# Local attention: GpSimd normalises q as well as k, and VectorE's product of the maxima with q's reciprocal norm is gone

## What is computed

```python
def l2norm(t):
    return t / jnp.clip(jnp.linalg.norm(t, axis=-1, keepdims=True), 1e-12)

h = shift_token(x)
q, k, v = jnp.split(h @ wqkv, 3, axis=-1)        # 8 heads of 64
q = l2norm(q) * qs
k = l2norm(k) * ksc
q, k = rotary_xpos(q, k)
bq = q.reshape(b, h, w, WINDOW, d) * QK_SCALE    # windows of 64 tokens
sim = einsum(bq, own and previous window of k)   # causal mask, 128 keys at most
attn = jax.nn.softmax(sim, axis=-1)
x = x + (attn @ v) @ wo
```

## Time and profile before

| | us |
|---|---|
| median of 3 runs | 1655.27 (1651.87 to 1656.19) |
| the profiled execution, its own time | 1658.24 |
| its span in the trace | 1656.5 |
| PE busy | 1525.9 (92%) |
| DVE busy | 1137.0 (69%) |
| ACT busy | 1083.1 (65%) |
| POOL busy | 517.0 (31%) |

### The profile page before, as it was taken

How to read it: one execution, slowest core, us unless ns; L and a number is a source line. 1 busy time by engine, 2 the same in 40 slices (tenths; PEclk the granted TensorE clock), 3 DMA queues, 4 the chain that set the end, 5 groups by cost and what they waited for, 6 DMA issues and landing times. The chain is left out here.

```text
span 1656.5 us, 30452 instructions
## 1 busy us (share of the span) xinstructions
PE 1525.9 (92%) x10190; PEld 1033.3 (62%) x10190; DVE 1137.0 (69%) x2336; ACT 1083.1 (65%) x2499; POOL 517.0 (31%) x476
## 2 busy tenths in 40 slices
PE   7999999999979999999979999996999888999986
PEld 6777777777667888888854333333566555566654
DVE  2666666666658777777787788864677654767755
ACT  2555555555567888888856577754777755777751
POOL 1222222222232112222110000015767633776732
PEclk9999999999979999999987799978999999999998
DMA  7000000000011221221100000000000000000000
GB/s 236 2 2 0 0 0 0 0 0 0 1 49 57 77 76 64 76 76 55 59 1 1 1 1 1 1 1 1 1 1 1 1 1 0 1 2 1 1 1 26
DMA packets 18993, 36.35 MB, mean 22 GB/s; under 512 B 5764, under 2 KB 11008, under 8 KB 16704
## 3 DMA queue, kind: packets, MB, share of 16 engines
q1 hardware_dynamic: 18896, 35.09, 6.4%
HBM read 33.91 MB, written 1.18 MB: 21 GB/s over the span
## 5 line engine op out<-in xcount | busy, mean ns | idle before, releaser
L915 DVE TENSOR_TENSOR m_hidp<-m_hid,m_hidp 128x512 fp32r<-128x512 f32 x256 | 181.6, 737 | 76.6 <-ACT m_hidp L831 75.4
L305 ACT ACTIVATE a_prob<-ps,a_negmax 128x512 f32<-128x512 f32 (+3 forms) x256 | 134.0, 526 | 146.7 <-DVE a_negmax L381 146.7
L836 ACT ACTIVATE m_hid<-ps,pre_w 128x512 f32<-128x512 f32 x256 | 175.7, 687 | 63.2 <-PE ps L1064 62.5
L1064 PE MATMUL ps<-c_sb_st,m_w1p 128*128 128x512 f32 x768 | 192.1, 399 | 0.0
L1119 PE MATMUL ps<-m_hidp,m_w2p 128*128 128x512 f32 x768 | 190.0, 396 | 0.2 <-DVE m_hidp L915 0.2
L1441 ACT ACTIVATE c_sb_pT<-ps 128x512 f32<-128x512 f32 x256 | 137.4, 601 | 79.6 <-PE ps L1654 78.6
L1511 DVE TENSOR_REDUCE c_sb_negmax<-ps 128x1 f32<-128x512 f32 x240 | 152.7, 684 | 47.2 <-PE ps L1639 47.1
L265 POOL TENSOR_TENSOR a_qk_r<-a_qk_c,a_qk_s 128x512 f32<-128x512 f32 x64 | 81.3, 1270 | 324.0 <-DVE a_qk_s L372 324.0
L2039 ACT ACTIVATE l_sb_prob<-ps,l_sb_negmax,l_sb_rn 128x192 f32<-128x192 f32 (+1 forms) x256 | 124.1, 494 | 69.5 <-DVE l_sb_negmax L2140 69.5
L1064 PEld LDWEIGHTS ps<-c_sb_st,m_w1p 128*128 128x128 f32 x768 | 145.5, 190 | 37.8 <-issue 3.0
L1119 PEld LDWEIGHTS ps<-m_hidp,m_w2p 128*128 128x128 f32 x768 | 144.1, 188 | 35.8 <-DVE m_hidp L915 0.4
(11 more groups left out here) (247 smaller groups left out, 3253.9 us busy)
## 6 DMA issues: line engine op xcount, KB each, us to landing
m_gate_all<-m_gates_d SPq DMA_DIRECT2D x16, 1024.0 KB, 4.7
pre_w<-w1T SPq DMA_DIRECT2D x14, 258.0 KB, 2.6
pre_w<-w2T SPq DMA_DIRECT2D x14, 256.0 KB, 2.7
pre_wqkv<-wqkv SPq DMA_DIRECT2D x2, 768.0 KB
keep_x<-x SPq DMA_DIRECT2D x1, 1024.0 KB, 10.0
out<-keep_x SPq DMA_DIRECT2D x4, 256.0 KB, 2.5
keep_xT<-xT SPq DMA_DIRECT2D x1, 768.0 KB, 5.2
pre_m_w<-l_w SPq DMA_DIRECT2D x2, 341.0 KB
```

The costliest lines, as they stand in the source:

```text
L305: nc.scalar.activation(prob[:, u % 4, 0:width(p)], score_ps(b, p, j)[:, 0:width(p)], ACT.Exp, bias=negmax[:, u:u + 1], accum_out=den[:, b ...
L836: nc.scalar.activation(hid[:, c % 2, f, :], ps[:, f, :], ACT.Gelu, bias=w1[:, k, FF + f:FF + f + 1]).then_inc(gelu_done, 1)
L915: nc.vector.tensor_tensor(hidp[:, c % 2, 1, f, :], hid[:, c % 2, f, :], hidp[:, c % 2, 0, f, :], ALU.subtract).then_inc(low_done, 1)
L1064: ins = nc.tensor.matmul(ps[:, f, :], w1p[:, k, a, f * P:(f + 1) * P], xp[:, b, c, :], start=(i == 0), stop=(i == 2))
```

## The change

`norms` on GpSimd now does for q what it did for k. It computes the reciprocal norms of q, multiplies the rotated q with them in place, and then does the same two steps for k. So the power for k comes after the whole of q, where before it came first. `turn_qk` for q waits for the normalised q. On VectorE the instruction L2140 goes, with its waits, and `rowmax` writes `negmax` directly. On ScalarE the exponential keeps its bias and has no scale operand. `rn` is kept for one tile only.

```diff
-            nc.gpsimd.tensor_tensor(rn[:, t, NH2:2 * NH2], ssqc[:, NH2:2 * NH2], neg_half[:, 0:NH2], ALU.pow
-                                    ).then_inc(rn_step, 1)
-            pool.wait_ge(rope_add, n + 1)
-            pool.wait_ge(rn_step, 2 * n + 1)
-            wait_past(pool, qkT_mm, 2 * n)
-            nc.gpsimd.tensor_tensor(k_n[:, :].rearrange("p (h d) -> p h d", d=HD2),
-                                    qk_r[:, 1, :].rearrange("p (h d) -> p h d", d=HD2),
-                                    rn[:, t, NH2:2 * NH2, None].broadcast_to([P, NH2, HD2]), ALU.mult
-                                    ).then_inc(qk_norm, 1)
-            nc.gpsimd.tensor_tensor(rn[:, t, 0:NH2], ssqc[:, 0:NH2], neg_half[:, 0:NH2], ALU.pow
-                                    ).then_inc(rn_step, 1)
-            pool.wait_ge(rn_step, 2 * n + 2)
+            for w in range(2):
+                nc.gpsimd.tensor_tensor(rn[:, heads(w)], ssqc[:, heads(w)], neg_half[:, 0:NH2], ALU.pow
+                                        ).then_inc(rn_step, 1)
+                if w == 0:
+                    pool.wait_ge(rope_add, n + 1)
+                else:
+                    wait_past(pool, qkT_mm, 2 * n)
+                pool.wait_ge(rn_step, 2 * n + w + 1)
+                nc.gpsimd.tensor_tensor((k_n[:, :] if w else qk_r[:, 0, :]).rearrange("p (h d) -> p h d", d=HD2),
+                                        qk_r[:, w, :].rearrange("p (h d) -> p h d", d=HD2),
+                                        rn[:, heads(w), None].broadcast_to([P, NH2, HD2]), ALU.mult
+                                        ).then_inc(qk_norm, 1)
...
-                                           bias=negmax[:, u:u + 1], scale=rn[:, t, u:u + 1], accum_out=den[:, t % 2, u:u + 1])
+                                           bias=negmax[:, u:u + 1], accum_out=den[:, t % 2, u:u + 1])
...
-            nc.vector.tensor_reduce(negraw[:, us],
+            nc.vector.tensor_reduce(negmax[:, us],
...
-                                    else blocks(t, ps[:, 2 + k % 2, 0:2 * KEYS]), AX.X, ALU.max, negate=True).then_inc(raw_max, 1)
-            dve.wait_ge(raw_max, PAIRS * n + k + 1)
-            dve.wait_ge(rn_step, 2 * n + 2)
-            nc.vector.tensor_tensor(negmax[:, us], negraw[:, us], rn[:, t, us], ALU.mult).then_inc(max_done, 1)
+                                    else blocks(t, ps[:, 2 + k % 2, 0:2 * KEYS]), AX.X, ALU.max, negate=True).then_inc(max_done, 1)
...
-            pe.wait_ge(qk_norm if w else rope_add, n + 1)
+            pe.wait_ge(qk_norm, 2 * n + w + 1)
```

More of the change, by code:

```diff
@@ L1860, in local_attention @@
     ssqc = sb("ssqc", [P, 2 * NH2])
-    rn = sb("rn", [P, TPB, 2 * NH2])
+    rn = sb("rn", [P, 2 * NH2])
     neg_half = sb("neg_half", [P, 2 * NH2])
@@ L1869, in local_attention @@
     v = sb("v", [P, TPB, INNER])
-    negraw = sb("negraw", [P, NH2])
     negmax = sb("negmax", [P, NH2])
@@ L1900, in local_attention @@
     s_mm = sem("s_mm")
-    raw_max = sem("raw_max")
     max_done = sem("max_done")
@@ L1955, in norms, with heads @@
         def norms(n, t):
+            def heads(w):
+                return slice(w * NH2, (w + 1) * NH2)
             pool.wait_ge(ssq_done, n + 1)
-            nc.gpsimd.tensor_tensor(rn[:, t, NH2:2 * NH2], ssqc[:, NH2:2 * NH2], neg_half[:, 0:NH2], ALU.pow
-                                    ).then_inc(rn_step, 1)
-            pool.wait_ge(rope_add, n + 1)
-            pool.wait_ge(rn_step, 2 * n + 1)
-            wait_past(pool, qkT_mm, 2 * n)
-            nc.gpsimd.tensor_tensor(k_n[:, :].rearrange("p (h d) -> p h d", d=HD2),
-                                    qk_r[:, 1, :].rearrange("p (h d) -> p h d", d=HD2),
-                                    rn[:, t, NH2:2 * NH2, None].broadcast_to([P, NH2, HD2]), ALU.mult
-                                    ).then_inc(qk_norm, 1)
-            nc.gpsimd.tensor_tensor(rn[:, t, 0:NH2], ssqc[:, 0:NH2], neg_half[:, 0:NH2], ALU.pow
-                                    ).then_inc(rn_step, 1)
-            pool.wait_ge(rn_step, 2 * n + 2)
+            for w in range(2):
[10 more added lines that the diff above has]
+                                        ).then_inc(qk_norm, 1)
         def widen(n):
```

## The result

| | before | after |
|---|---|---|
| median of 4 runs, us | 1653.57 (1650.82 to 1656.19) | 1751.55 (1749.44 to 1758.99) |
| ratio to before | | 1.0595, 95% interval 1.0572 to 1.0618 |
| profiled execution, us | 1658.24 | 1749.6 |
| its span, us | 1656.5 | 1747.8 |
| mean granted TensorE clock | 0.961 | 0.937 |

The forecast was 1704 with a range of 1690 to 1721. The sign was right, the size was not: the change costs 98 us where 49 were forecast, and the time lies outside the range.

What follows compares the result with a forecast made beforehand. TensorE was taken to bound the kernel, any delay of k's transpose delaying the step. Terms 31.0 + 14.9 + 2.5 + 2.8 + 0.5 less 2.0 and 0.6 gave +49 us on 1655.3: 1704, range 1690 to 1721.

Steps and rivals of the forecast that it cites:

- the order: GpSimd's queue: q's multiplication and k's power now precede k's multiplication, so k's transpose starts later; 43 of the 49 us.
- the collision with t = 0: In seven steps VectorE's rope_c starts 0.19 before GpSimd's multiplication of k, making k 0.86 later; 6 us.
- The path to k: From GpSimd's first multiplication (q) through k's power and multiplication to TensorE's weight load for k: 3.93 us.
- 1.41 us later: TensorE's transpose of k starts 1.41 us later in 22 of 30 steps, and each step pays it in full.
- the rival at 1698: GpSimd also starts before rope_c in steps with t = 0, so no collision costs anything; 6 us less, chance 0.21.
- GpSimd is first by 0.14 ... which costs nothing: In steps of three windows GpSimd's multiplication of k starts 0.14 before VectorE's rope_c, which waits at no cost.
- a rival with a chance of 0.15: rope_c also beats GpSimd's multiplication of k in twelve steps like step 7, 1.17 each; 14 us more, 1718, chance 0.15.
- TensorE's clock falls ... 11 us more: Rival: TensorE's longer pause before k lowers its clock to 0.79 for 5 us of eight worst steps; 1715, chance 0.10.
- I cost it at nothing: Dropping VectorE's small product and the exponentials' scale operand gains nothing in 30 steps, since TensorE then waits for k.
- faster: Rival: k is ready before TensorE needs it, pair 2's transposes come 0.51 earlier per step; 15 us won, 1640, chance 0.04.
- no change: Rival: GpSimd's loss just eats VectorE's gain, needing k 2.5 us after GpSimd's first multiplication starts; chance 0.03.

Runs made afterwards that it cites:

- one_power: The changed kernel with one GpSimd power over all 16 heads of q and k before both multiplications; 1656.02 us, ratio 1.0010.
- both: The changed kernel with VectorE's rope_c behind the output's addition and one unread TensorE product ahead of k's transposes; 1685.17 us, ratio 1.0195.

## Why the prediction found only half of the loss

The 49 us of the forecast were 43 for the order and 6 for the collision with t = 0, and nothing for the clock. The traces show 33, 28 and 35.

**The path to k: right.** 3.93 us was forecast from the start of the first multiplication to k's weight load, and 3.94 and 3.93 were measured where nothing collides. The change moves a power of 1.64 and a multiplication onto the path that sets every step.

**"1.41 us later" in each step: too high by 0.26.** Without collision and at full clock a step of three windows is 13.79 and not 14.05. Behind a late k the transposes of pair 3 follow at once, since their exponentials are long done: in one_power they start 0.46 after k's, in the kernel before 0.60. From k's weight load to the output projection pass 1.10 us in the kernel before (1244.43 to 1245.53) and 0.82 with a late k (1246.80 to 1247.62 in "both"), which is the 0.26. Over 29 steps it makes 7.5 us. The forecast without any collision had 43 (the rival at 1698), 3.3 of them in the first step of the first layer, ahead of the measured stretch: 43 - 3.3 - 7.5 = 32, where the traces show 33 for the order.

**"GpSimd is first by 0.14 ... which costs nothing": wrong, 22 us by itself.** This is the step that failed first. The margin was 0.06, and a margin of this size is none: by the records GpSimd starts first and loses. I had written the other outcome down as a rival with a chance of 0.15, but at 14 us. I gave it twelve steps like step 7; the trace shows all 20 of three windows that have a `rope_c`, at 1.09 each (2.13 against 1.04), 22 us. With the steps of t = 0, which the sum did hold (6 us at 0.86 each, 0.78 by the record), that is 27, against 28 by the traces and 35, give or take 7, by the ratios.

**"TensorE's clock falls ... 11 us more": the mechanism right, the size wrong, and it was not in the sum.** It measured 30 us by the medians and 35 by the traces. I priced eight worst steps, since I took the two rivals one at a time. With the collision gone it is 11 us, as I had priced it (eight output projections are slow there, four of them in steps with t = 0). Together with the collision the pause is 2.84 us and not 1.6 in steps of three windows, and then the clock of whole stretches averages 0.86. The output projection alone pays 0.86 us there (1.92 against 1.06). The Trainium skill (TensorE: Matmul & The Clock Gate, Part 1) ties the clock to recent activity; the two kernels with products in the pause agree: more work, a clock back at 0.99, and 35 and 11 us less from the first to the last output projection.

**"I cost it at nothing": true here as far as the traces go, and a gain of some 30 us overlooked.** The removal on VectorE and ScalarE is worth 32 us by the medians and 27 by the traces as soon as k is on time, most of it by the product. I had it in the rival "faster", at 15 us (0.51 a step, with pair 2 alone). The step won 0.79, because pair 3 and the projection behind it move up too. That its value here was nothing because k came later still is argued from TensorE's waits; no run has the late k together with the product.

**The rival "no change"** said that no row of GpSimd's is short enough. That was true of the rows and false of the kernel: one power of 16 heads takes 2.90 where two of 8 take 3.28, and it ends only 0.2 us behind `rope_sum` (1224.89 + 2.90 against 1227.57). Its time was 1656.

## What to carry to other kernels

Before an operation is moved to the engine that seems idle, list what is queued between the release and the result that others wait for, and put on that stretch only what needs the late input; what can be computed earlier (here the power) goes ahead of it. Two estimates of start times that differ by 0.1 us are a tie: price the lost race in every step, not in those where the sum says so. And price rivals together where one lengthens the pause on which the other hangs, TensorE's clock above all.

## What the runs showed of the hardware

- **A race is not decided by the start in the records.** GpSimd's multiplication of 128x512 lost to VectorE's product of two SBUF tensors with 0.06 us of lead and won with 0.14, 0.19 and 0.26. The loser ends almost its whole duration behind the winner (0.91 of 1.04). The Trainium skill (SBUF — State Buffer, SBUF: two separate sides) calls the shared pair of ports a lock, held for the whole instruction by whoever starts first. The traces agree on the lock; on the start they agree only where the lead is 0.14 or more, if the start is taken from the records. What decides at 0.06 stays open.
- **GpSimd's power** takes 1.64 us for 128x8 and 2.90 for 128x16: 0.16 an element and some 0.38 for the instruction, if those two are on a line; a third, of 128x4 elsewhere in the changed kernel, takes 1.02 and lies on it. The multiplication of 128x512 takes 1.04. In one step of the changed kernel the power of 128x8 starts 0.12 behind `rope_sum` and takes 2.59, so it can lose a race too. During a power that is under way VectorE's small instructions ran at their usual times; during a multiplication a product of 128x2 took 0.64 in place of 0.16, and a clamp of 128x16 beside `rope_s` took 0.73 in place of 0.17.
- **Adding work made a kernel faster three times:** by the medians three reciprocals a step by 42 us, three products by 30, one product by 16 (by the traces 43, 35 and 11).
